# A transformer block on one core: the context's norm with tokens on partitions, made on GpSimd during self-attention, and cross-attention's first K inside the norm of x

## What is computed

```python
def _adaln(x, c, lw, lb, gw, gb, bw, bb):
    return _ln(x, lw, lb) * (1.0 + (c @ gw + gb)) + (c @ bw + bb)
def _attn(xq, ctx, wq, wkv, wo, bo):       # 16 heads of 64
    q = rope(heads(xq @ wq)); k, v = split(ctx @ wkv); k = rope(heads(k)); v = heads(v)
    return concat(softmax(q @ k.T * 64 ** -0.5) @ v) @ wo + bo
x = _attn(_adaln(x, ..ln1), same, sa..) + x                   # self-attention, 256 keys
ctx_n = _ln(context, ca_lnc_w, ca_lnc_b)                      # the context's norm
x = _attn(_adaln(x, ..ln1), ctx_n, ca..) + x                  # cross-attention, 1601 keys
x = gelu(_adaln(x, ..ln2) @ ff_w1 + ff_b1) @ ff_w2 + ff_b2 + x
```

## Time and profile before

| | us |
|---|---|
| median of 3 runs | 2123.01 (2122.61 to 2126.22) |
| the profiled execution, its own time | 2127.94 |
| its span | 2126.2 |
| granted TensorE clock, mean | 0.974 |
| busy: PE, DVE, POOL, ACT | 2008.8, 1622.6, 1174.4, 990.0 |

### The profile page before, as it was taken

One profiled execution on the slowest core, in us unless ns is written; L12 is line 12 of the kernel. 1 busy time (PEld: TensorE's weight loads), 2 busy tenths in 40 slices (PEclk: granted clock), 3 DMA queues, 4 the chain that ended last, 5 costly groups with the idle time before them and its releaser, 6 DMA issues.

```text
span 2126.2 us, 53808 instructions
## 1 busy us (share of the span) xinstructions
PE 2008.8 (94%) x20816; PEld 1346.6 (63%) x20816; DVE 1622.6 (76%) x2362; ACT 990.0 (47%) x1606; POOL 1174.4 (55%) x721
## 2 busy tenths in 40 slices
PE   5899999879699999999999999999999999999987
PEld 2666667622166666666666766767666776776653
DVE  3788888836578888888887888888788887888832
ACT  2344444424244445445445545444554544554533
POOL 1344444400056667677677667667666766766760
PEclk8999999979799999999999999999999999999999
DMA  3522222100011111111111111111111111111100
GB/s 112 165 80 75 81 79 82 54 0 1 32 55 54 47 54 60 47 54 57 50 52 55 54 49 54 58 47 54 60 47 54 59 48 53 55 53 52 48 22 20
DMA packets 109750, 118.69 MB, mean 56 GB/s; under 512 B 26432, under 2 KB 74688, under 8 KB 109248
## 3 DMA queue, kind: packets, MB, share of 16 engines
q1 hardware_dynamic: 109504, 115.27, 16.4%
HBM read 36.52 MB, written 1.05 MB: 18 GB/s over the span
## 4 chain that ended last, share of the span: by engine, by line
PE 68%; POOL 13%; issue 11%; DMA 3%; DVE 3%; ACT 2%; SPq 0%; POOLq 0%; ACTq 0%; DVEq 0%
PE S L1089 18%; PE OB L1101 16%; PE PB L1036 8%; PE PB L1047 8%; PE S L1062 6%; POOL psum_acc L503 4%; POOL psum_acc L470 4%; POOL KL L463 4%; PE S L885 2%; PE PB L1110 2%; DMA qswapped<-qturned 2%; PE PB L1026 1%; PE PB L872 1%; PE PB L1120 1%; PE PB L1071 1%
## 5 line engine op out<-in xcount | busy, mean ns | idle before, releaser
L503 POOL TENSOR_TENSOR psum_acc<-psum_acc,P 124x1024 f32<-124x1024 f32 (+1 forms) x320 | 689.4, 2154 | 92.9 <-ACT P L628 75.1
L628 ACT ACTIVATE P<-S 124x1024 f32<-124x1024 f32 (+1 forms) x448 | 431.3, 963 | 465.9 <-PE S L1089 465.1
L817 DVE TENSOR_REDUCE mxc<-S 128x2 f32<-128x1024 f32 x384 | 469.1, 1222 | 89.4 <-PE S L1062 88.6
L1101 PE MATMUL OB<-P,V 124*64 124x256 f32 (+1 forms) x3328 | 429.4, 382 | 0.0
L496 POOL TENSOR_TENSOR psum_acc<-P 124x1024 f32<-124x1024 f32 x64 | 152.3, 2379 | 331.4 <-ACT P L628 331.4
L1101 PEld LDWEIGHTS OB<-P,V 124*64 124x64 f32 (+1 forms) x3328 | 224.5, 137 | 131.0 <-issue 40.8
L1089 PE MATMUL S<-QH,KH 64*124 64x256 f32 (+1 forms) x1664 | 254.2, 301 | 3.0 <-ACT P L628 3.0
L783 DVE TENSOR_TENSOR turned<-PB,rope 128x512 f32<-128x512 f32 (+1 forms) x256 | 146.0, 570 | 120.6 <-PE PB L1036 120.2
L1089 PE MATMUL S<-QL,KH 64*124 64x256 f32 (+1 forms) x1664 | 234.8, 277 | 0.0
L1089 PE MATMUL S<-MX,share 64*124 64x256 f32 (+1 forms) x1664 | 234.7, 277 | 0.0
L1089 PE MATMUL S<-QH,KL 64*124 64x256 f32 (+1 forms) x1664 | 234.5, 277 | 0.0
(11 more groups left out here) (118 smaller groups left out, 3241.2 us busy)
## 6 DMA issues: line engine op xcount, KB each, us to landing
swapped<-turned SPq DMA_DIRECT2D x512, 128.0 KB, 2.1
kv_w<-sa_kv_dram SPq DMA_DIRECT2D x64, 128.0 KB, 2.3
qswapped<-qturned SPq DMA_DIRECT2D x128, 64.0 KB, 1.9
kv_w<-ca_kv_dram SPq DMA_DIRECT2D x64, 96.0 KB, 2.2
ctxT_all<-ctxT_dram SPq DMA_DIRECT2D x8, 600.4 KB, 5.3
q_w<-sa_wq_dram SPq DMA_DIRECT2D x64, 64.0 KB, 2.0
q_w<-ca_wq_dram SPq DMA_DIRECT2D x64, 64.0 KB, 2.0
o_w<-ca_wo_dram SPq DMA_DIRECT2D x64, 64.0 KB, 2.1
```

The costliest lines, as they stand in the source:

```text
L503: pool.tensor_tensor(acc, acc, P_of(J, c)[0:rows, :, 0:w], ALU.add).then_inc(x.acc, 1)
L628: act.activation(P_of(J, c)[0:rows, :, 0:w], SP[0:rows, :, 0:w], ACT.Exp, scale=SCALE).then_inc(x.e, 1)
L817: dve.tensor_reduce(mxc[:, t, :, c:c + 1], MP[:, :, 0:w], AX.X, ALU.max).then_inc(x.am, 1)
L1101: ins = pe.matmul(OB[half(h), 0:N], Vb[J % 2][0:w, t, half(h)], P_of(J, c)[0:w, h, k * N:(k + 1) * N], start=(t == 0), stop=(t == len(a_.t ...
```

## The change

The context's norm no longer stands between LN2 and cross-attention. The context is loaded with tokens on partitions: 13 tiles of 128 tokens x 96 features for each batch (the last tile holds 65 tokens), 1248 columns per batch, in the upper part of the same tile `ctxT_all`, now 128 partitions high. In this form mean and variance are sums along the free axis.

- **POOL** sums by a tree of additions over halves (`tree`, two batches of a group g together: 48, 24, 12, 6, 3 columns per tile and then one), subtracts the mean (`centre`) and multiplies by the reciprocal (`scale`) with operands that are repeated along the features. One group's tree has 8 additions (and one multiplication for a mean) in 6 pieces, `centre` and `scale` have 4 instructions of 7 or 6 tiles each. The first two groups' means and centring come before the self-attention loop; the rest is an `agenda` of pieces, of which the words `cp` (after `l`) and `cq` (after `f`, every other iteration) issue three in two iterations, from iteration 3 on.
- **ACT** squares a batch (128 x 1248) in iterations 0, 1, 4, 5, 19, 20, 31, 32, takes the roots of 52 columns in iterations 12 and 39 (word `cn`), and after each turned group applies scale and bias from PSUM into `ctxT_all` (word `ca`).
- **DVE** takes the reciprocals of 52 columns in iterations 13 and 40 (`cn`).
- **PE** turns up to four tiles (128 x 96) in each of iterations 24 to 39 and 45 to 60 by products with `ident` into bank `OB` (word `ct`); every fourth of these turns a single tile of 65 tokens. `p` waits until ACT has read the turned tiles.
- **SP** loads the context of batches 0 to 3 with the weights of steps 0 and 1 and those of 4 to 7 with the weights of steps 2 to 5; `rope` is loaded in four parts after the swaps of steps 44 to 47 (its tile serves as scratch for the squares until then).
- The word lists of self-attention change beside that: `v` moves ahead of `sum` on PE, and ACT's list is turned round to `e mr+1 ca cn ve+3 h+3 oe`.
- **LN2** moves into `cross`. The norm of x uses bank `SP` for means and spread; the first two K chunks of cross-attention's step 0, with their rotation, stand between its words on PE, DVE, ACT and SP, and the first weights of cross-attention are loaded once self-attention's last V is done. The first q waits for `LN2.done`.

```diff
     SELF = Stage("sa",
-                 "qk+3 sum+-1 p+-1 s v+2 a+2 m+1 o+-1",
-                 "r+2 am+1 t+3 rc+-1 dv+-1 c+3 ad+-1",
-                 "ve+1 mr h+2 oe+-1 e",
-                 "l+2 f",
+                 "qk+3 v+2 sum+-1 p+-1 s a+2 ct m+1 o+-1",
+                 "r+2 am+1 t+3 rc+-1 dv+-1 c+3 ad+-1 cn",
+                 "e mr+1 ca cn ve+3 h+3 oe",
+                 "l+2 cp f cq",
                  "w+3 x+2")
...
+        def tokens(b):
+            return ctxT_all[:, TOK + b * CW:TOK + (b + 1) * CW].rearrange("p (t c) -> p t c", c=DC)
+        def over(stat, lo, hi):
+            return stat[:, lo:hi].rearrange("p (t a) -> p t a", a=1).broadcast_to([D, hi - lo, DC])
+        ROPE = 44
+        SQUARES = {0: 0, 1: 1, 4: 2, 5: 3, 19: 4, 20: 5, 31: 6, 32: 7}
+        ROOTS = {12: 0, 39: 1}
+        INVERSES = {13: 0, 40: 1}
+        TURNS = {J: n for n, J in enumerate(list(range(24, 40)) + list(range(45, 61)))}
+        BLOCKS = [("sum", 0), ("sum", 1), ("var", 0), ("var", 1), ("sum", 2), ("sum", 3), ("var", 2), ("var", 3)]
...
+                for b in ((0, 1), (2, 3), (4,), (5,), (6,), (7,))[J] if J < 6 else ():
+                    sp.dma_start(ctxT_all[:, TOK + b * CW:TOK + (b + 1) * CW], ctx_in[:, b * CW:(b + 1) * CW]
+                                 ).then_inc(cx.load[b], 16)
 
             def self_swap(J, _):
                 i = J % SLOTS
                 wait(sp, z.t, J + 1)
                 for k in range(2):
                     sp.dma_start(swapped[i][k::2, :], turned[i][1 - k::2, :]).then_inc(z.swap[i], 16)
-                if J < B:
-                    sp.dma_start(ctxT_all[:, J * M:(J + 1) * M], ctxT_in[:, J * M:(J + 1) * M]).then_inc(s_ctx, 16)
                 if J == B:
-                    sp.dma_start(cols96[:], cols96_in).then_inc(s_ctx, 16)
-                    sp.dma_start(rope[:], rope_in[:, 0:2 * M]).then_inc(s_ctx, 16)
+                    sp.dma_start(cols96[:], cols96_in).then_inc(s_cols, 16)
+                if ROPE <= J < ROPE + 4:
+                    lo, hi = ((J - ROPE + i) * M // 2 for i in range(2))
+                    sp.wait_ge(cx.tree, tree_end("var", B // 2 - 1, 2))
+                    sp.dma_start(rope[:, lo:hi], rope_in[:, lo:hi]).then_inc(s_rope, 16)
 
...
+            sp.wait_ge(z.v, STEPS)
+            for J in range(2):
+                cross_weights(J, J)
+            for c in range(2):
+                swap_k(0, c)
             sp.wait_ge(z.added, B)
-            sp.wait_ge(LN2.done, NLN)
-            sp.wait_ge(LNX.done, NCL)
             run_steps(a_, in_order(a_.sp, {"q": swap_q, "k": swap_k, "w": cross_weights_of,
-                                              "wo": cross_out_weights_of}))
+                                              "wo": cross_out_weights_of},
+                                   [("w", 0, 0), ("w", 0, 1), ("k", 0, 0), ("k", 1, 0)]))
 
...
+            def tree(what, g, piece):
+                at = tree_end(what, g, 0)
+                out = (cmean if what == "sum" else cstd)[:, 2 * g * CT:2 * (g + 1) * CT].rearrange(
+                    "p (t a) -> p t a", a=1)
+                if piece < 2:
+                    b = 2 * g + piece
+                    wait(pool, cx.tree, at)
+                    if what == "sum":
+                        pool.wait_ge(cx.load[b], 16)
+                        source = tokens(b)
+                    else:
+                        wait(pool, cx.squared, b + 1)
+                        source = csq[piece][:, :, :]
+                    half = DC // 2
+                    pool.tensor_tensor(ctree[:, piece * CT:(piece + 1) * CT, :], source[:, :, 0:half],
+                                       source[:, :, half:DC], ALU.add).then_inc(cx.tree, 1)
+                for n, (levels, w) in enumerate((((2,), (24,)), ((3,), (12,)), ((4, 5), (6, 3)))):
+                    if piece == n + 2:
+                        for level, w in zip(levels, w):
+                            pool.wait_ge(cx.tree, at + level)
+                            pool.tensor_tensor(ctree[:, :, 0:w], ctree[:, :, 0:w], ctree[:, :, w:2 * w], ALU.add
+                                               ).then_inc(cx.tree, 1)
+                if piece == 5:
+                    pool.wait_ge(cx.tree, at + 6)
+                    pool.tensor_tensor(out, ctree[:, :, 0:1], ctree[:, :, 1:2], ALU.add).then_inc(cx.tree, 1)
+                    pool.wait_ge(cx.tree, at + 7)
+                    pool.tensor_tensor(out, out, ctree[:, :, 2:3], ALU.add).then_inc(cx.tree, 1)
+                    if what == "sum":
+                        pool.wait_ge(cx.tree, at + 8)
+                        cols_g = slice(2 * g * CT, 2 * (g + 1) * CT)
+                        pool.tensor_scalar(cmean[:, cols_g], cmean[:, cols_g], 1.0 / DC, None, ALU.mult
+                                           ).then_inc(cx.mean, 1)
+            def quarter(g, piece):
+                b, cuts = 2 * g + piece // 2, (0, (CT + 1) // 2, CT)
+                return b, cuts[piece % 2], cuts[piece % 2 + 1]
+            def centre_context(g, piece):
+                b, lo, hi = quarter(g, piece)
+                part = tokens(b)[:, lo:hi, :]
+                pool.wait_ge(cx.mean, g + 1)
+                pool.tensor_tensor(part, part, over(cmean, b * CT + lo, b * CT + hi), ALU.subtract
+                                   ).then_inc(cx.centred, 1)
+            def scale_context(g, piece):
+                b, lo, hi = quarter(g, piece)
+                part = tokens(b)[:, lo:hi, :]
+                pool.wait_ge(cx.inv, g // 2 + 1)
+                pool.wait_ge(cx.squared, b + 1)
+                pool.tensor_tensor(part, part, over(cstd, b * CT + lo, b * CT + hi), ALU.mult).then_inc(cx.unit, 1)
...
+                agenda = [p for block in (("var", 0), ("var", 1), ("sum", 2), ("centre", 2), ("scale", 0), ("scale", 1),
+                                          ("sum", 3), ("centre", 3), ("var", 2), ("var", 3)) for p in pieces(*block)]
+                agenda += [None] * 7 + pieces("scale", 2) + pieces("scale", 3)
+                def context_first(J, _):
+                    n = (J - 3) // 2 * 3 + (J - 3) % 2 * 2
+                    if 0 <= n < len(agenda) and agenda[n]:
+                        context_piece(*agenda[n])
+                def context_second(J, _):
+                    n = (J - 3) // 2 * 3 + 1
+                    if (J - 3) % 2 == 0 and 0 <= n < len(agenda) and agenda[n]:
+                        context_piece(*agenda[n])
 
...
-                run_steps(SELF, in_order(SELF.pool, {"l": low_parts, "f": fold}))
+                run_steps(SELF, in_order(SELF.pool, {"l": low_parts, "f": fold, "cp": context_first,
+                                                     "cq": context_second}))
...
+            for block_ in (("sum", 0), ("centre", 0), ("sum", 1), ("centre", 1)):
+                for p in pieces(*block_):
+                    context_piece(*p)
...
+                def context_squares(J, _):
+                    if J in SQUARES:
+                        b = SQUARES[J]
+                        g = b // 2
+                        wait(act, cx.centred, 2 * b + 2)
+                        if g > 0:
+                            wait(act, cx.tree, tree_end("var", g - 1, b % 2 + 1))
+                        act.activation(csq[b % 2][:, :, :], tokens(b), ACT.Square).then_inc(cx.squared, 1)
+                    if J in ROOTS:
+                        g = 2 * ROOTS[J]
+                        columns = slice(g * 2 * CT, (g + 2) * 2 * CT)
+                        wait(act, cx.tree, tree_end("var", g + 1))
+                        act.activation(cstd[:, columns], cstd[:, columns], ACT.Sqrt, bias=epsc[:, :], scale=1.0 / DC
+                                       ).then_inc(cx.std, 1)
+                def context_out(J, _):
+                    if J in TURNS:
+                        b, g = TURNS[J] // CG, TURNS[J] % CG
+                        at, w = b * M + 4 * g * D, min(4 * D, M - 4 * g * D)
+                        if TURNS[J] == 0:
+                            act.wait_ge(s_cols, 16)
+                        wait(act, cx.turned, TURNS[J] + 1)
+                        act.activation(ctxT_all[0:DC, at:at + w], OB[0:DC, 0:w], ACT.Identity,
+                                       scale=cols96[:, 0:1], bias=cols96[:, 1:2]).then_inc(cx.done, 1)
...
+                do = {"qh": high_q, "kh": high_k, "ve": read_v, "mr": rows_of_max, "e": exponentials, "oe": read_o}
+                norm(LN2, 0, "square0 square1 square2 square3 root kh0 kh1 out0 out1 out2 out3", first(do, "kh"))
+                run_steps(a_, in_order(a_.act, do, [("kh", 0, 0), ("kh", 1, 0)]))
...
+                def context_inverse(J, _):
+                    if J in INVERSES:
+                        g = 2 * INVERSES[J]
+                        columns = slice(g * 2 * CT, (g + 2) * 2 * CT)
+                        wait(dve, cx.std, g // 2 + 1)
```

(30 more changed lines are left out.)

252 lines of the change are left out of this document (114 added, 138 removed).

## The result

The changed kernel takes 2025.33 us, the median of 4 runs (2021.4 to 2029.9), against 2122.81 us (2121.7 to 2126.22) for the kernel before on the same chip: a ratio of 0.9541 [0.952, 0.9562]. It is faster by 97.5 us. The forecast was 2041, the range 2020 to 2074. The profiled execution took 2026.98 us, with a span of 2025.2 and a mean granted clock of 0.981.

A forecast was written before the change was run, and what follows sets the result against it. PE bounds cross-attention; DVE paces self-attention, PE close behind; the gain lies between them. -103 - 4 + 4 + 18.5 + 3 = -81.5 from 2127.94 gives 2046.4; with the median 4.9 lower, 2041, range 2020 to 2074.

The forecast's parts named there:

- A: Between self-attention and cross-attention's first scores: context norm off the path, first K inside LN2, -103 us (bounds -98 to -111).
- D: Turning tiles on TensorE in self-attention: 0.97 us more per four tiles, steps of 5.95, +18.5 us (bounds +15.5 to +33).
- C: GpSimd's norm pieces in self-attention: longer pieces make `f` late by 0.3 us, +4 us in all (bounds 0 and +18).
- B: Context loads at self-attention's start: spreading them gives back two thirds of 6.4 us excess, -4 us (bounds -9 and +2).
- E: Squares, roots with four table loads on ScalarE, reciprocals on VectorE, in self-attention: +3 us (bounds 0 and 7).
- rival 4: GpSimd far slower on short runs, factor f on its pieces, prologue +28 or +36: 2155 us at 2.5; chance 0.03.
- 1: Rival: TensorE's weight loads don't hide in the turning, 0.39 us a tile, +33 instead of +18.5: 2056 us; chance 0.12.
- 2: Rival: GpSimd becomes the bound in self-attention, pieces costing 1.5 times what long rows say, +22: 2063 us; chance 0.12.
- 3: Rival: the turned group's scale and bias on ScalarE needs another table than `e`, +18 to +42: about 2070 us; chance 0.07.
- 5: Rival: removing the norm brings less, as K's weights, `rope` or swaps also held cross-attention up; no chance of its own.
- LN2 begins near 460, within 10: Sign of being right: in the new trace LN2 starts near 460 us (438.9 - 4 + 4 + 18.5 + 3), within 10.
- the 5.95: Sign of being right: self-attention steps near 5.95 us in the turning, 5.2 to 5.5 outside it.

The follow-up runs named there:

- before_again: The kernel before, unchanged, run and profiled a second time: 2122.43 us.
- old_lists: The changed kernel with the old word orders on PE and ACT, the new work kept in: 2037.45 us, 0.9592 of the kernel before.
- small_pieces: The changed kernel with nearly every GpSimd piece of the context's norm cut to one tile: 2023.7 us, 0.9536 of the kernel before.
- after: The first profile of the changed kernel itself, nothing further changed: the profiled execution took 2026.98 us.
- h_first: The changed kernel with `h` ahead of `ve` in ACT's list: 2019.56 us (0.9512 of the kernel before), and 2024.49 us (0.9531) in 5 rounds.
- before_lists: The kernel before with only the two new word orders on PE and ACT: 2121.57 us, 0.9981 of the kernel before.

## Why the prediction was right, point by point

The direction, the cause and the size of the main term were right; the forecast of 2041 was 15.7 us too slow. By the profiled executions' own times it is 19.4 (2046.4 against 2026.98); the 3.7 between the two come from the medians, 4.9 below the profiled execution before and 1.65 below it after. The 19.4 are 17 in self-attention (+21.5 forecast, +4.45 measured) and 2.5 behind it.

- **A, -103: right.** Measured -105.15 against the profiled execution before, and -99.8 against before_again, where the way to q ran at a better granted clock (0.93 for 0.86); both lie in the bounds of -98 to -111. q comes 20.7 us behind `xT` (22.5 expected), the spreads 15.4 (10.7 + 3.4 expected), scores 6.4 behind q (6.3 expected). The granted clock fell twice. It is 0.63 from 458 to 462, behind PE's 4.34 us of waiting for the reciprocal, and 0.94 from 462 to 466. From 470 to 494 it is 0.50, the lower of its two levels (1.2 GHz), behind 4.91 us of waiting for q's high part. That gives 0.92 up to q and 0.59 behind it, as before.
- **D, +18.5: the step that failed.** The turning stretches cost +8. The price of a group was right: 1.05 us measured, 0.97 taken, 0.22 a tile. What was wrong is the sentence "PE's step becomes 4.98 + 0.97 = 5.95": 4.98 was read from a trace in which `v` stands between `s` and `a`, and the change moves `v`. In the new order PE's own work is 4.67, and the step measures 5.60. With the old order the sum would have held: old_lists takes 6.07 a step, and from `e` 24 to 40 and 45 to 61 it is 8.5 and 9.05 us above the kernel before, +17.5. The prediction named the new order only for its effect on waits. Old_lists differs from the changed kernel in nothing but the two orders, and the weight loads put 0.35 of its 0.47 us a step down to the place of `v`; 0.12 stand at `sum` and `p` with ACT's old order. D is 10.5 of the 17 us.
- **C, +4: nearly nothing.** small_pieces, with almost none of the norm's GpSimd work, takes the same time, and the same from `e` 8 to 61 within 1 us. The durations of long-run pieces were right or too high. The argument that `f` would be 0.3 us late left out that a late `f` need not matter once `v` stands ahead of `sum` and fills PE's wait; that reason is argued, the nil is shown. The rule of the Trainium skill, "GPSIMD Engine Reference", section 7, does not hold for these additions: runs of 48 to 3 columns took 1511 to 342 ns, the time of long runs by the column.
- **B, -4: near right, but not in the first profile.** There `e` 0 comes 3.8 us later than before, `e` 0 to 8 gives back 2.6, and `e` 8 starts at 100.5, 1.2 later. That pair misleads: `e` 8 starts at 99.3, 101.0 and 99.9 in the three profiles without the change, and at 95.2 to 98.3 in all with it but after and old_lists. `e` 0 to 8 takes 41.8 to 45.2 us in the changed kernel and its variants with the new orders, 47.9 and 46.9 in the kernel before. The start depends on where LN1 ends: its bias add starts at 32.7 and 34.3 in the two profiles of the kernel before, at 32.4 to 34.9 in the others. From there to `e` 0 it is 18.8 to 19.8 us in the four profiles with ACT's old order and 20.5 to 21.2 in the seven with ACT's new one that aren't h_first's, so about 1.5 us of the late start come with ACT's new order.
- **E, +3: about right.** Steps 13 and 40, with the roots, are 1.0 and 0.8 us longer; steps 5 and 21, with squares, 0.3 to 0.4, which the prediction held for nothing. All stay in small_pieces, so they are ScalarE's or VectorE's. The roots brought four table loads of 1.28 us, as predicted.
- **Not foreseen:** `e` 8 to 24 got 3.2 us shorter in spite of C and E. The new orders do it: before_lists, without anything else of the change, has 2.85 of it. The irregular steps of the old order are fewer there; the earlier trace rows shows only a regular step, and I read no more than that and the batch's mean.
- **Readings that were off without effect:** the hole in POOL's strip is three slices wide and not five. The rows at 8.12 were taken at half clock, but the profile's record of the clock only begins at 13.9, so no run shows that. By its own formula 26 (f-1), rival 4's prologue costs 31 and 39 us, not 28 and 36.

The rivals: 1 is out (0.22 a tile, not 0.39), 2 and 4 are out (pieces at 1.0 times or less, small_pieces equal), 3 is out (no load at L706), 5 is out (53.6 us from the last add to the first exponential instead of 158.7 or 153.3). The sign "LN2 begins near 460, within 10" failed at 443.3, by D, C and the new orders' effect on `e` 8 to 24; of the others the 5.95 failed, and a few steps outside the turning took over 5.5 us (13: 6.25, 44: 5.72).

## What to carry to other kernels

A busy time belongs to the order in which it was read: when a change moves a group of matmuls as well as adding one, price the move too, by looking at what each group costs behind its neighbours, start to start. Groups whose weights have the same shape belong together. The second-tightest engine is where an edit of order pays: alone it was worth 0.2%, with new work on that engine 11 to 14 us. A serial stretch can be spread over an engine that is half empty, in pieces about as long as its gaps, and here that cost nearly nothing. Take a second profile of the kernel before too: its hand-over alone varied by 5.4 us, its start by 2.6.
